# Whitening a 64-channel image on one core: the last stage's products on quarters of the array, and another mapping of rows to partitions

## The reference, cut to what matters

```python
# layer 0: group norm (32 groups of 2 channels), spectral convolution, residual
x = x + _L0_conv_ref(_gn(x), L0_conv_weight_re, L0_conv_weight_im, L0_conv_bias)
# layer 1: group norm, whitening over groups of 16 of the last axis (the 256 columns), residual
x = x + _L1_conv_ref(_gn(x))

def _L1_conv_ref(x):                       # c = 256 columns, groups of M = 16
    f = x_flat - mean                      # per column, over everything else
    cov = (1 - EPS) * einsum('gmn,gkn->gmk', fg, fg) / denom + EPS * eye
    chol = cholesky(cov / denom)
    inv_sqrt = solve_triangular(chol, eye, lower=True)
    return einsum('gmk,gkn->gmn', inv_sqrt, fg)
```

## Time and profile before

| | us |
|---|---|
| median of 3 runs | 3913.86 (3909.84 to 3916.74) |
| the profiled execution | 3919.83 |
| its span, first to last instruction | 3918.0 |
| TensorE's mean granted clock | 0.935 of 2.4 GHz |
| busy: PE, PEld, DVE, ACT, POOL | 3335.6, 2521.1, 2456.9, 1637.1, 1396.4 |
| the last stage, first product to the end | 1870 to 3918 |

### The profile page before, as it was taken

How to read it: one execution, slowest core, us unless ns; L and a number is a source line. 1 busy time by engine, 2 the same in 40 slices (tenths; PEclk the granted TensorE clock), 3 DMA queues, 4 the chain that set the end, 5 groups by cost and what they waited for, 6 DMA issues and landing times.

```text
span 3918.0 us, 157070 instructions
## 1 busy us (share of the span) xinstructions
PE 3335.6 (85%) x60165; PEld 2521.1 (64%) x60165; DVE 2456.9 (63%) x3911; ACT 1637.1 (42%) x3624; POOL 1396.4 (36%) x1690
## 2 busy tenths in 40 slices
PE   4888888888887331564999999999999999999999
PEld 3555555555554331222788888888888888888888
DVE  4989889898898437555455555555555555555555
ACT  1434334343343221000455555555555555555554
POOL 3656666666666113453222222222222222222221
PEclk7989999999999555898999999999999999999999
DMA  9999999999998661996788888888888888888887
GB/s 213 302 279 304 298 290 303 292 305 289 289 299 236 89 88 13 305 355 198 237 262 263 263 264 262 263 263 263 263 262 263 263 263 263 263 263 263 263 262 252
DMA packets 1023610, 1001.96 MB, mean 256 GB/s; under 512 B 103728, under 2 KB 988608, under 8 KB 1023552
## 3 DMA queue, kind: packets, MB, share of 16 engines
q1 hardware_dynamic: 995904, 917.19, 78.4%
q10 hardware_dynamic: 27648, 83.90, 8.5%
HBM read 639.66 MB, written 361.28 MB: 255 GB/s over the span
## 4 chain that ended last, share of the span: by engine, by line
PE 66%; DVE 13%; issue 10%; DMA 5%; ACT 2%; POOL 2%; SPq 1%; DVEq 1%; POOLq 0%; another core or an unknown queue 0%; ACTq 0%
PE bank L627 23%; PE bank L612 11%; PE bank L602 11%; PE bank L616 6%; DVE reg L873 4%; DMA reg<-gram_d 4%; PE bank L442 4%; PE bank L453 3%; DVE reg L866 3%; DVE gmask L889 2%; PE bank L461 2%; PE bank L539 2%; PE bank L477 1%; ACT xh L663 1%; SPq L308 1%
## 5 line engine op out<-in xcount | busy, mean ns | idle before, releaser
L627 PEld LDWEIGHTS bank<-wp,xt_sb 128*128 128x128 f32 x8192 | 993.1, 192 | 256.5 <-issue 256.4
L663 ACT ACTIVATE xt_sb<-bank 128x512 f32<-128x512 f32 x1024 | 611.5, 597 | 947.8 <-PE bank L616 908.1
L1090 DVE SCALAR_TENSOR_TENSOR v_r<-v_h,tab,bank 102x512 fp32r<-102x512 f32 x512 | 382.8, 748 | 984.0 <-ACT v_h L663 984.0
L627 PE MATMUL bank<-wp,xt_sb 128*128 128x128 f32 x8192 | 996.2, 275 | 0.0
L780 POOL TENSOR_TENSOR reg<-reg 128x512 f32<-128x512 f32 x512 | 747.1, 1461 | 504.0 <-PE bank L453 411.7
L833 POOL TENSOR_TENSOR wp<-wr,tab 128x256 f32<-128x256 f32 x512 | 327.8, 640 | 1606.3 <-PE bank L627 1599.9
L1097 DVE SCALAR_TENSOR_TENSOR o_sb<-bank,m,mwhit 128x512 f32<-128x512 f32 x1024 | 718.9, 744 | 3.4 <-PE bank L627 3.1
L873 DVE TENSOR_TENSOR reg<-xh 128x128 f32<-128x128 f32 x1024 | 602.9, 627 | 147.9 <-ACT xh L663 133.1
L612 PE MATMUL bank<-tab,reg 128*128 128x128 f32 x4096 | 615.7, 272 | 0.0
L602 PE MATMUL bank<-tab,cs 128*102 128x512 f32 x1024 | 525.4, 594 | 1.7 <-DVE ey_r L1082 1.7
L612 PEld LDWEIGHTS bank<-tab,reg 128*128 128x128 f32 x4096 | 497.0, 140 | 37.3 <-issue 1.9
(11 more groups left out here) (124 smaller groups left out, 2258.7 us busy)
## 6 DMA issues: line engine op xcount, KB each, us to landing
reg<-in_x_dram SPq DMA_DIRECT2D x256, 1024.0 KB, 9.3
reg<-in_x_dram SPq DMA_DIRECT2D x512, 512.0 KB, 3.8
out_dram<-o_sb SPq DMA_DIRECT2D x512, 512.0 KB, 3.2
xh_d<-xh ACTq DMA_DIRECT2D x128, 512.0 KB
reg<-xh_d SPq DMA_DIRECT2D x128, 512.0 KB, 5.9
gram_d<-gram ACTq DMA_DIRECT2D x64, 256.0 KB
reg<-gram_d SPq DMA_DIRECT2D x64, 256.0 KB, 4.8
spec_d<-psu SPq DMA_DIRECT2D x512, 8.5 KB
```

The costliest lines, as they stand in the source:

```text
L627: ins = mm(bank[4 + 2 * e + c][:, W * r + P * half:W * r + P * half + P], xt_sb[:, e, half, H * c + P * r:H * c + P * r + P], wp[:, e, hal ...
L663: copy = lambda o, i, **k: nc.scalar.activation(o, i, ACT.Copy, **k)
```

## The change

Two things are changed, both in the last stage.

1. `whitened`: each 128 x 128 product becomes four pairs of 64 x 64. `rows` picks the upper or lower 64 partitions of both operands, which are 64 of the 128 columns of the image, `cols` picks 64 of the 128 rows of the image in the stationary tile and with it the half of PSUM's partitions that the result goes to. Since `wp` is block diagonal with blocks of 16, the 64 x 64 blocks off its diagonal are zero, and are not computed. There are 32 products per pair in place of 8, by the same count 64 instructions in place of 16. [...] The parity of the pair no longer picks a bank, so the wait for `o_ready` asks for the result two half pairs back (`c - 1` for `c - 3`, with a head start of 1 for 4). PE increments a new semaphore, `o_begun`, behind that wait. DVE reads two banks for a half pair, so it has four instructions of 128 x 256 per pair in place of two of 128 x 512, with `rows` picking every second run of 64 in `o_sb` and in `mwhit` (now two copies side by side).
2. `load` and `store` use the layout `(p t)`: rows 2p and 2p + 1 lie on partition p, and a packet is two rows, 2 KB. The order of the rows in the constant table `hb` follows.

The diff, without the line that adds the name `o_begun`:

```diff
@@ -71,7 +71,8 @@
     for par in range(2):
         ew[:, par, :, 0:(KY + 1 - par) // 2] = wj.reshape(2, KY, W)[:, par::2, 0:P].transpose(2, 0, 1)
     put("ew", ew)
-    hb = hk_row[:, None, :] * (chan[:, None] == np.arange(2))[:, :, None]
+    by_parity = hk_row.reshape(P, H // 2, 2).transpose(0, 2, 1).reshape(P, H)
+    hb = by_parity[:, None, :] * (chan[:, None] == np.arange(2))[:, :, None]
     put("hb", hb.reshape(P, 2 * H))
     put("e0", cj[:, None] * wj, slice(0, KW))
     put("e1", cj[:, None] * wj, slice(1, KW + 1))
@@ -140,7 +141,8 @@
     ds = bass.ds
     x_v = x.rearrange("b c (t p) w -> p (b c) t w", p=P)
-    out_v = out.rearrange("b c (t p) w -> p (b c) t w", p=P)
+    x_rows = x.rearrange("b c (p t) w -> p (b c) t w", p=P)
+    out_rows = out.rearrange("b c (p t) w -> p (b c) t w", p=P)
     xh_d = nc.dram_tensor("xh_d", (NU, P, PAIRS, W), f32, kind="Internal").ap()
@@ -228,7 +230,7 @@
         qt, qtp = sb("qt", [KW, KW + 1]), sb("qtp", [KW, P])
         cov, covg = sb("cov", [P, 2 * BL]), sb("covg", [P, 2 * BL])
         fac = sb("fac", [M, M])
-        whit, msum, mwhit = sb("whit", [P, 2, P]), sb("msum", [P, 2, P]), sb("mwhit", [P, W])
+        whit, msum, mwhit = sb("whit", [P, 2, P]), sb("msum", [P, 2, P]), sb("mwhit", [P, 2, W])
         with nc.sbuf_tensor("spectrum", [P, NP * KW], f32) as reg1:
             D, _ = cut(reg1, 0, NP, KW)
@@ -258,7 +260,7 @@
                                 x_re_used0=1, x_re_used1=1, x_re_used2=1, x_re_used3=1, xh_mm=2),
                     scalar=dict(dt_copied=1, xh_copied=2, xt_copied=2, gram_copied=2, rot2_act=4, xt2_copied=2, xh_out0=1,
                                 xh_out1=1, gram_out=1, out_stored0=1, out_stored1=1, out_stored2=1, out_stored3=1),
-                    vector=dict(xw_made=5, v_split=2, d_copied=1, diag_done=1, rot_read=1, q_read=2, o_ready=4),
+                    vector=dict(xw_made=5, v_split=2, d_copied=1, diag_done=1, rot_read=1, q_read=2, o_ready=1),
                     gpsimd=dict(gram_used=2, w_ready=2))
         START = {name: k for starts in HEAD.values() for name, k in starts.items()}
         S = {n: sem(n) for n in names}
@@ -399,11 +401,11 @@
             sp.wait_ge(*nth("ms_ready", 1))
             def load(t, j):
-                sp.dma_start(x_re[:, 2 * j:2 * j + 2], x_v[:, ds(t * 8 + 2 * j, 2)]).then_inc(S[f"x_re_in{j}"], 16)
+                sp.dma_start(x_re[:, 2 * j:2 * j + 2], x_rows[:, ds(t * 8 + 2 * j, 2)]).then_inc(S[f"x_re_in{j}"], 16)
             def store(t, j):
                 sp.wait_ge(*nth("o_ready", t * 8 + 2 * j + 2))
-                sp.dma_start(out_v[:, ds(t * 8 + 2 * j, 2)],
+                sp.dma_start(out_rows[:, ds(t * 8 + 2 * j, 2)],
                              o_sb[:, j].rearrange("p (c r) w -> p c r w", c=2)).then_inc(S[f"out_stored{j}"], 16)
             for j in range(4):
@@ -621,12 +623,17 @@
                 pe.wait_ge(*nth("w_ready", t * 4 + q + 1))
                 pe.wait_ge(*nth("xt2_copied", t * 8 + 2 * q + 2))
                 for c in range(2):
-                    pe.wait_ge(*nth("o_ready", t * 8 + 2 * q + c - 3))
+                    pe.wait_ge(*nth("o_ready", t * 8 + 2 * q + c - 1))
+                    pe.sem_inc(S["o_begun"], 1)
                     for r in range(2):
                         for half in range(2):
-                            ins = mm(bank[4 + 2 * e + c][:, W * r + P * half:W * r + P * half + P],
-                                     xt_sb[:, e, half, H * c + P * r:H * c + P * r + P], wp[:, e, half],
-                                     start=r == 0 and half == 0, stop=True, skip_group_check=True)
+                            for rows in range(2):
+                                k = slice(KH * rows, KH * rows + KH)
+                                for cols in range(2):
+                                    h0, at = H * c + P * r + KH * cols, P * r + KH * half
+                                    ins = mm(bank[4 + 2 * c + rows][KH * cols:KH * cols + KH, at:at + KH],
+                                             xt_sb[k, e, half, h0:h0 + KH], wp[k, e, half, KH * rows:KH * rows + KH],
+                                             start=r == 0 and half == 0, stop=True, skip_group_check=True)
                             if c == 0 and r == 0 and half == 0:
                                 ins.then_inc(S[f"x_re_used{q}"], 1)
                     ins.then_inc(S["o_mm"], 1)
@@ -733,7 +740,8 @@
             copy(msum[:, :, :].rearrange("p a b -> p (a b)"), bank[3][:, 0:W]).then_inc(S["ms_ready"], 1)
             root(act, 3, root_in[0:M, 0:M])
             act.wait_ge(*nth("mw_mm", 1))
-            copy(mwhit[:, :], bank[4][:, 0:W], scale=1.0 / ROWS).then_inc(S["mw_ready"], 1)
+            copy(mwhit[:, :, :], bank[4][:, 0:W].unsqueeze(1).to_broadcast([P, 2, W]),
+                 scale=1.0 / ROWS).then_inc(S["mw_ready"], 1)
             def scaled(t, q):
                 act.wait_ge(*nth("w_ready", t * 4 + q - 1))
                 copy(wr[:, q % 2].rearrange("p a b -> p (a b)"), flat(whit[:, :, :]),
@@ -1094,12 +1102,15 @@
                 dve.wait_ge(*nth(f"out_stored{q}", t * 16))
                 for c in range(2):
                     dve.wait_ge(*nth("o_mm", t * 8 + 2 * q + c + 1))
-                    v.scalar_tensor_tensor(
-                        out=o_sb[:, q, 2 * c:2 * c + 2],
-                        in0=bank[4 + 2 * (q % 2) + c][:, :].rearrange("p (r w) -> p r w", r=2),
-                        scalar=m1[:, ds(t * 4 + q, 1)],
-                        in1=mwhit[:, :].unsqueeze(1).to_broadcast([P, 2, W]),
-                        op0=ALU.add, op1=ALU.subtract).then_inc(S["o_ready"], 1)
+                    by_rows = lambda a: a.rearrange("p r (f k w) -> p k (r f) w", f=2, k=2)
+                    for rows in range(2):
+                        ins = v.scalar_tensor_tensor(
+                            out=by_rows(o_sb[:, q, 2 * c:2 * c + 2])[:, rows],
+                            in0=bank[4 + 2 * c + rows][:, 0:W].rearrange("p (g w) -> p g w", w=KH),
+                            scalar=m1[:, ds(t * 4 + q, 1)],
+                            in1=by_rows(mwhit[:, :, :])[:, rows],
+                            op0=ALU.add, op1=ALU.subtract)
+                    ins.then_inc(S["o_ready"], 1)
             def four(t, first=False, last=False):
                 for q in range(4):
```

More of the change, by code:

```diff
@@ L251, in whiten_kernel @@
             ms_mm ms_ready mw_mm mw_ready
-            cs_ready w_scaled w_ready x_re_in0 x_re_in1 x_re_in2 x_re_in3 v_mm ey_in ey_high ey_ready v_high v_split xt2_mm xt2_copied o_mm o_ready x_re_used0 x_re_used1 x_re_used2 x_re_used3
+            cs_ready w_scaled w_ready x_re_in0 x_re_in1 x_re_in2 x_re_in3 v_mm ey_in ey_high ey_ready v_high v_split xt2_mm xt2_copied o_begun o_mm o_ready x_re_used0 x_re_used1 x_re_used2 x_re_used3
             out_stored0 out_stored1 out_stored2 out_stored3""".split()
```

## The result

| | before | after |
|---|---|---|
| median, us | 3915.3 (4 runs) | 3665.78 (3656.86 to 3670.25, 4 runs) |
| ratio, 95% interval | 1 | 0.9361 [0.934, 0.9383] |
| the profiled execution, us | 3919.83 | 3668.49, its span 3666.7 |
| a pair in the last stage, us | 3.98 | 3.50 |

The forecast was 3571 with a range of 3470 to 3725. The kernel became faster, by 250 us where 343 were expected. The gain is in the last stage, 0.48 us for each of the 512 pairs, and so is what is missing of it.

What follows compares the result with a forecast made beforehand. PE was taken to bound the last stage: whitening 1.78 to 1.11 us (products 0.93, tile changes 0.18), times 512, saves 343 us; 3919.8 becomes 3577, median 3571. Bounds 3458 to 3725; 3470 to 3725 held about 82%.

Steps and rivals of the forecast that it cites:

- PE is the bound, and 0.1 us of a pair is 51 us: Last stage: PE always busy, 3.98 us a pair, 512 pairs; 0.1 us is 51 us if nothing else is later.
- The part it fell into (3640 to 3725, 16%): Upper part of the range: DMA as the bound at 296 GB/s, together with an array at 17.8 ns a step; 16%.
- The products: Whitening: 64 quarter-array instructions, four at a time, 14.5 ns a step, 0.93 us a pair (0.89 to 1.14).
- rival 1: Whitening: tiles sharing output partitions run two at a time, 27.8 ns a step, 92 us slower, 4006 us; 10%.
- Rival 2: Whitening: a fixed step of 25 ns an instruction, so no change, 3914 us; 3%.
- rival 6: Whitening: loads take turns with products of the same rows, 1004 us slower, 4918 us; 1%.
- The change of tile: Whitening between whole-array products: 0.09 us for each change of tile, two in a pair, 0.18 us.
- The sign that the steps beside the whitening would stay at 0.44, 0.23 and 0.86: PE's chain, last stage: transposes 0.44, product 0.23 and `expand` 0.86 us stay unchanged beside a whitening of 1.0 to 1.2.
- PE's other 2.20 us: Last stage: everything in PE's pair besides whitening stays untouched at 2.20 us, so a pair takes 3.31 us.
- `o_begun` and the middle of the pair: Whitening: if products run out at the increment of `o_begun`, one more 0.09 us; in the upper end only.
- the 0.9 us of cover in the prediction: DVE, last stage: first half's results end 2.45 us after `expand`, PE wants them at 3.31, covered by 0.9 us.
- Without longer packets this would be a tie: DMA, last stage: 317 GB/s needed at 3.31 us a pair, just what the engines give with the present packets.

Runs made afterwards that it cites:

- The two rotated runs: Changed kernel with the same order of work, PE's loop cut behind `expand` in place of behind the whitening, run twice: 3621.46 us (0.9277) and 3616.38 us (0.9285).
- the move of `expand`: Changed kernel with `expand` moved behind the whitening in each pair, DVE's order as before: 4422.33 us, 1.1377 to the kernel before.

## Why the prediction was right, and where its sum was off

- *PE is the bound, and 0.1 us of a pair is 51 us.* Right. The two halves done alone show it: products alone 0.9367, mapping alone 1.0, and in neither does PE wait for another engine.
- *The number.* 3666 lies in the range, but above the 3500 to 3640 that had 62%. The part it fell into (3640 to 3725, 16%) had been meant for DMA as the bound and an array at 17.8 ns a step, and neither came. The mechanism was right. That the range, drawn for these other terms, was wide enough for the two misses below is luck.
- *The products.* Taken at 14.5 ns a step, measured 14.6, with the products done twice and by the rounds of four. One quarter alone needs 58.4 ns, so four of them lose nothing. The unknown behind it, two row tiles that give to the same partitions of PSUM in two banks, did not hold anything up: rival 1 would have shown a step of 27.8. Rival 2, 25 ns, and rival 6, loads in turn with products, are out by the same number: four products begin 6 to 7 ns apart, and the 64 loads lie beside them, 1.02 us beside 1.16.
- *The change of tile.* This term was mis-sized. It was read from one step, from a 128-column transpose to a 32-column product, and used for both ways. Entry is 0.09, as taken (0.86 to 0.95 us). For the rest, the chain has 1.09 + 0.59 us for whitening and the transposes behind it; less the columns' 0.93, the entry's 0.09 and the transposes' 0.44 this leaves 0.22 where 0.09 was taken. 0.13 us x 512 is 67 us. The starts divide the 0.22: the second round is 0.05 late, the first transpose begins 0.11 later than one more round would, and the second transpose 0.165 us behind the first in place of 0.11. Something like the last of these stood in the kernel before: in its first stage, behind the 32-column products of line 453, line 461's second product begins 0.165 us after its first (the median of some 500), where line 612's do so after 0.11. The sign that the steps beside the whitening would stay at 0.44, 0.23 and 0.86 failed for this reason.
- *What the sum did not have.* The loop's end. The prediction said that PE's other 2.20 us were untouched. But the time in which PE's instruction stream works off its branch (0.61 us from the loop's end to the transposes) had been hidden by long products, and 0.26 us of it came out, once in four pairs: 126 x 0.26 = 33 us. The two rotated runs give 33 and 34 us. 67 + 33 = 100 us, and 3571 + 100 = 3671 stands beside 3666 measured.
- *`o_begun` and the middle of the pair.* The upper end had one more 0.09 for it. It costs nothing: the step over it is 38 to 39 ns, as between any two rounds.
- *DVE.* Four results take 1.65 us in the timeline against 1.72 taken, one 0.476 alone. It did not become the bound (0.66 busy), and the two-deep banks held. How near they are to not holding is what the move of `expand` showed: the 0.9 us of cover in the prediction is real, and a change of PE's order that uses it up costs 14%.
- *DMA.* The prediction reckoned with a need of 317 GB/s; 299 were needed, and 305 in the rotated kernel. "Without longer packets this would be a tie" is for 317, and no kernel here asks for that much; at 305 GB/s and a share of 0.98 nothing is lost yet.

## What to carry to other kernels

Independent products that are block diagonal in both operands can be put on quarters of the array. Here, with neighbours in the program on different quarters, the products' part of a pair went from 1.78 to 0.93 us, where half would be 0.89 (the two halves of the rows also go to different banks, and no run changes that); with eight in a row on one quarter the whitening took 2.62 us. But each visit to the small tiles costs about 0.3 us here (0.09 + 0.22), so it wants many products a visit. When instructions become short, look at what their length was hiding: here the end of a loop on the same engine cost 33 us behind the short products, and nothing once it stood behind the longest work, two products of 0.43 us. And before an order is changed in a pipeline written by hand, count the time from a product to the results that its successor waits for, on all engines between.

## What was not expected of the hardware

- PE does not begin its products strictly in the order of the program. With eight instructions on a quarter in a row, the next quarter's first begins while three of the eight have not begun (at 3001.965 us, 6 ns after the fifth). In the changed kernel the two instructions of one product use the same quarter, and still the first round has the first instruction of every quarter (all four take 0.267 us) and the others, by their 58.4 ns, one of each; if the two lie side by side in PE's stream, the fourth product's first begins ahead of three others, too. No trace here shows an instruction passing more than three. How the two lie in the stream is not recorded.
- When a loop's end behind the whitening is worked off, PE has only 16 to 18 products and 12 to 17 loads still to begin, whether a product's step is 111 ns (17), 41 (18) or 14.6 (16). With other work before the branch it is fewer (ten in the rotated kernel); what sets the number is not shown.
- The price of the small tiles is not the same both ways: 0.09 us on entry, about 0.2 in all for the first steps and the way out; of it 0.15 lies in what comes behind if that is the four transposes, and 0.17 if it is `expand`.
- Longer packets lowered the share of the DMA engines from 0.83 to 0.77 at 263 GB/s, and no time came of it up to a share of 0.98.
